# Preact convolution pair, one core: the work in front of the sampling loop in another order

## The chip, the core and the metric

The kernel runs on one core of a Trainium2 chip. Its time is the device time of one execution in microseconds (us), the median of several executions. The engines that matter are TensorE (PE), VectorE (DVE), ScalarE (ACT), GpSimd (POOL) and SyncE (SP, which here only issues DMAs). Each engine runs its own instructions strictly in the written order; they meet through semaphores.

## The reference

Two residual blocks on x of shape 4 x 128 x 32 x 32 (images, channels, rows, columns), in float32. Only the first concerns the change:

```python
def _gn(v, G=32, eps=1e-05):              # group norm without weights, 32 groups
    g = v.reshape(B_, G, C_ // G, H_, W_)
    m = jnp.mean(g, axis=(2, 3, 4), keepdims=True)
    s = jnp.var(g, axis=(2, 3, 4), keepdims=True)
    return ((g - m) / jnp.sqrt(s + eps)).reshape(v.shape)

x = x + _L0_conv_ref(_gn(x), ...)         # deformable 3x3 convolution, group norm of 16 groups
x = x + _L1_conv_ref(_gn(x), ...)         # two ternary 3x3 convolutions with batch norm

# inside _L0_conv_ref, x being the normalised input:
om = _conv2d(x, w_off, b_off, STRIDE, PAD)            # 27 channels: 9 taps x (y, x, mask)
off_y, off_x, m = jnp.split(om, 3, axis=1)
mask = jax.nn.sigmoid(m)
...                                                   # 4 bilinear corners, 9 taps, every pixel
out = jnp.einsum('bckhw,ock->bohw', sampled * mask[:, None], weight.reshape(Cout, Cin, KK))
```

## The kernel before

**Stages.** In front of the loop, up to about 41 us of the trace, the kernel loads x, normalises the four images, computes the offset convolution and writes the transposed images to DRAM (tensor xt), so that small patches of them can be fetched. Then a loop of 36 slots, 9 a image, samples and applies the deformable weights; then come the second block's convolutions. The change is in the first stage alone; nothing of the loop or of what follows it is written differently.

**Precision.** A float32 operand is split in a high part that TensorE takes as it is (xhi, wdhi, woffT part 0) and a low part, the rest (xlo, wdlo, woffT part 1); products of the pairs are added. So each image needs `heads` (ACT writes xhi from x, scale and shift), `whole` (the normalised image xb, on ACT for images 0 and 1; `whole_late`, on DVE, for 2 and 3), and the low part xlo = xb - xhi (`tails` on DVE, semaphore xlo_ok; for image 3 `low_parts(3)` on POOL, semaphore xlo_pool).

**Statistics.** For image b, DVE computes `image_stats` (two halves of 512 columns with BN_STATS, L1455, and one BN_AGGR, L1463). TensorE adds the channels of a group with a product by a constant matrix (`group_mean`, L693). DVE turns this into deviations (`deviation`, L1413 to L1408), TensorE adds again (`group_square`, L698), ACT takes the root (`root`, L1099), and DVE makes scale and shift (`scale_shift`, L1433 to L1448). Images 2 and 3 share one such round, named by 2. PE's products for the means stand between those of the offset convolution, at places that the table `SUMS` gives.

**Offset convolution.** `offset_part(b, h, part)`, for image b and its half h, is 6 products of 512 columns on xhi (part 0) or 3 on xlo (part 1), all L741. ACT adds the bias (`tail`, tile omc, L1127), PE turns the result so that pixels lie on partitions (`turn_offsets`, 24 small transposes, L767), DVE adds three rows of it (`offsets`, tile omr, L1833), ACT takes the sigmoid of the masks (`masks`, L1139), SP copies omr to the neighbouring partitions (`replicate`, semaphore rep_in), and POOL makes from it the distances (tile hat, L562 and L565), which ACT clips (`hats`, L1144 and L1146), and their outer product vt (`outer`, L575 and L581), one for each slot of the loop. The waits of an offset_part:

```python
if (b, h, part) == (0, 0, 0):
    pe.wait_ge(xhi_top, 1)
elif not part:
    pe.wait_ge(xhi_ok, b + 1)
elif b == 0:
    pe.wait_ge(xlo_first, 1)
elif b == 3:
    pe.wait_ge(xlo_pool, 1)
else:
    pe.wait_ge(xlo_ok, b)
```

**Images to DRAM.** `turn_image(b)` (PE, L718) transposes xb, `pixels_hi(b)` (ACT, L1134) and `pixels_lo(b)` (DVE, L1828) split it into xtv, SP stores it.

**Weights.** PE turns the 9 taps of the offset weights (L680) and of the deformable ones (`turn_deformable`, L688, wd_raw); ACT and DVE split these (`deformable_hi`, `deformable_lo`, tiles wdhi and wdlo, L1803).

**The first products.** As soon as POOL has written the identity matrix, PE runs `keep_going(6)`, six products of the identity with itself (L672), whose result nobody reads; one more stands behind each of the first two group sums.

**Who orders the work.** Everything is an order written by hand, engine by engine. PE's, from image 1 on: offset_part(1,0,0) with both sums of images 2 and 3 in it, turn_offsets(0), offset_part(1,0,1), turn_image(1), offset_conv(1,1), turn_image(2), offset_conv(2,0), turn_offsets(1), turn_image(3), offset_conv(2,1), offset_conv(3,0), and then the first outer products. The sums of all images share one PSUM bank with the output of offset_part(1,1,0), which therefore waits for the scale_shift of images 2 and 3 (gn_var).

Of the kernel before, what the change touches and what calls it, by code (L numbers as in the profile page):

```python
# [20 lines left out]
BIG = 512  # L21
# [36 lines left out]
def build(nc, x, w_off, b_off, wd, bias, gamma, beta, w1, g1, be1, w2, g2, be2, out):  # L58
# [8 lines left out]
    with ExitStack() as ctx:  # L67
# [432 lines left out]
        def _(pool):  # L500
# [47 lines left out]
            def low_parts(b):  # L548

                pool.wait_ge(xn_late, b - 1)  # L550
                pool.wait_ge(xhi_ok, b + 1)
                g.tensor_tensor(inner(xlo, b), square(plain(b)), inner(xhi, b), ALU.subtract).then_inc(xlo_pool, 1)
# [74 lines left out]
            for n in range(-5, CHUNKS):  # L627
                if 0 <= n + 3 < CHUNKS:
                    outer(n + 3)
                if n + 5 < CHUNKS:  # L630
                    distances(n + 5)
                if n == -4:
                    low_parts(3)
                for i, level in FOLDED.get(n, ()):
# [31 lines left out]
        def _(pe):  # L666
            t = nc.tensor

            def keep_going(n):

                for _ in range(n):
                    t.matmul(PS[:, 5, 0:P], ident[:, :], ident[:, :], start=True, stop=True)  # L672

            pe.wait_ge(consts, 1)
            keep_going(6)
            pe.wait_ge(consts, 3)
# [76 lines left out]
            def turn_offsets(b):  # L753
# [5 lines left out]
                for step in range(K):  # L759
# [12 lines left out]
            SUMS = {(0, 0, 0): ((group_mean, 1, (2, 0)),), (0, 1, 0): ((group_square, 1, (0, 0)),),  # L772
                    (1, 0, 0): ((group_mean, 2, (0, 0)), (group_square, 2, (2, 1)))}

# [11 lines left out]
            offset_part(1, 0, 0)  # L786
            turn_offsets(0)
            offset_part(1, 0, 1)
            turn_image(1)
            offset_conv(1, 1)  # L790
# [286 lines left out]
        def _(act):  # L1077
# [224 lines left out]
            heads(GN0, 1)  # L1302
            whole(GN0, 1)
            tail(0)
            tail(1)
            pixels_hi(0)
            root(GN0, 2)
# [79 lines left out]
        def _(dve):  # L1387
# [422 lines left out]
            dve.wait_ge(x_in[1], 16)  # L1810
            image_stats(GN0, 1)
            deviation(GN0, 1)
            dve.wait_ge(xhi_ok, 1)
            dve.wait_ge(xn_ok, 1)
            d.tensor_tensor(inner(xlo, 0), square(plain(0)), inner(xhi, 0), ALU.subtract).then_inc(xlo_first, 1)
            scale_shift(GN0, 1)
            dve.wait_ge(x_in[2], 16)
            image_stats(GN0, 2, last=False)
            deformable_lo(0)
            dve.wait_ge(x_in[3], 16)  # L1820
            image_stats(GN0, 3)
            deformable_lo(1)
            deviation(GN0, 2)
            tails(GN0, 1)
# [10 lines left out]

            dve.wait_ge(pads, 11)
            deformable_lo(2)
            pixels_lo(0)
            offsets(0)
            offsets(1)  # L1840
            scale_shift(GN0, 2)
            whole_late(2)
# [151 lines left out]
```

## Time and profile before

| | |
|---|---|
| median of 3 executions | 272.83 us (272.41 to 274.51) |
| the profiled execution | 272.33 us, its span 270.6 us |
| TensorE busy | 244.2 us, 90% of the span |
| VectorE busy | 213.6 us, 79% |
| ScalarE busy | 171.9 us, 64% |
| GpSimd busy | 166.3 us, 61% |
| mean granted TensorE clock | 0.978 |

The time of an execution lies 1.7 us above the span, which runs from the first to the last instruction. Matmuls are pipelined, so a long busy time of PE says only that something stood in it; where a chain of waits runs through an engine, that engine sets the time there. Times of the trace count from the start of the span.

### The profile page before, as it was taken

The page shows a single profiled execution, that of the slowest core. Times are in us where ns is not written, and L with a number is a line of the kernel's source. Part 1 is how long each engine was busy: PE and PEld are TensorE (multiplying, and loading weights), DVE is VectorE, ACT ScalarE, POOL GpSimd, SP SyncE. Part 2 cuts the span into 40 slices and gives each one's busy share as a digit, 9 for nine tenths or more (in the row PEclk, how much of TensorE's full clock was granted, in tenths as well). Part 3 has the DMA queues.
Part 4 walks back from the last instruction along what each step waited for, and adds up shares of the span by engine and source line. Part 5 has one row for each costly group of instructions (what it writes and reads, how often), then busy time and mean ns, then how long its engine had stood idle before and what let it go on. Part 6 is the DMA issues. An engine that isn't in the chain of part 4 may idle for free.

```text
span 270.6 us, 5607 instructions
## 1 busy us (share of the span) xinstructions
PE 244.2 (90%) x1960; PEld 210.8 (78%) x1960; DVE 213.6 (79%) x473; ACT 171.9 (64%) x364; POOL 166.3 (61%) x217
## 2 busy tenths in 40 slices
PE   6989998999999899998998999899999999999800
PEld 6867666899988799897998888899987776777600
DVE  5599556989888999559979789985588787699493
ACT  2488756989779978877799778757216406630140
POOL 8000899999668788777668987486900601936051
PEclk9999999999999999999999999999999999999965
DMA  7925686544444422333323334300000000000016
GB/s 216 378 69 186 208 263 239 164 146 135 133 140 135 127 95 75 110 114 108 111 79 105 96 131 132 103 30 2 0 0 0 2 1 0 0 0 2 5 54 261
DMA packets 25593, 28.13 MB, mean 104 GB/s; under 512 B 2509, under 2 KB 23613, under 8 KB 25560
## 3 DMA queue, kind: packets, MB, share of 16 engines
q1 hardware_dynamic: 24912, 25.95, 29.3%
q10 hardware_dynamic: 648, 1.76, 1.8%
q8 instruction: 18, 0.29, 0.5%
q14 instruction: 15, 0.12, 0.1%
HBM read 19.87 MB, written 6.78 MB: 99 GB/s over the span
## 4 chain that ended last, share of the span: by engine, by line
PE 64%; DVE 22%; ACT 8%; issue 2%; DMA 1%; DVEq 0%
PE PS L949 13%; PE PS L855 6%; PE PS L741 5%; PE PS L808 5%; PE PS L857 5%; PE PS L856 5%; PE PS L837 5%; DVE slo L1556 5%; PE PS L984 4%; PE PS L838 4%; PE PS L839 4%; DVE vlo L1567 3%; DVE st L1455 3%; ACT vhi L1165 3%; PE PS L767 2%
## 5 line engine op out<-in xcount | busy, mean ns | idle before, releaser
L581 POOL TENSOR_TENSOR vt<-rowm,hat 128x1026 f32<-128x1026 f32 x36 | 70.8, 1966 | 25.9 <-PE PS L817 24.1
L1567 DVE TENSOR_TENSOR vlo<-PS,vhi 128x576 fp32r<-128x576 f32 (+2 forms) x88 | 50.1, 590 | 17.5 <-ACT vhi L1165 17.2
L1165 ACT ACTIVATE vhi<-PS 128x576 fp32r<-128x576 f32 (+2 forms) x88 | 43.8, 523 | 19.1 <-PE PS L839 19.0
L1556 DVE TENSOR_TENSOR slo<-PS,shi 114x512 fp32r<-114x512 f32 (+1 forms) x68 | 43.2, 675 | 6.3 <-ACT shi L1153 6.0
L855 PE MATMUL PS<-vhi,wdhi 128*128 128x256 f32 x144 | 43.4, 301 | 0.8 <-ACT xb L1172 0.7
L837 PE MATMUL PS<-shi,patch 114*128 114x288 f32 (+1 forms) x136 | 42.0, 309 | 1.0 <-DVE vlo L1567 0.6
L857 PE MATMUL PS<-vhi,wdlo 128*128 128x256 f32 x144 | 40.5, 281 | 0.0
L856 PE MATMUL PS<-vlo,wdhi 128*128 128x256 f32 x144 | 40.4, 281 | 0.0
L838 PE MATMUL PS<-slo,patch 114*128 114x288 f32 (+1 forms) x136 | 40.2, 296 | 0.0
L839 PE MATMUL PS<-shi,patch 114*128 114x288 f32 (+1 forms) x136 | 40.0, 294 | 0.0
L1153 ACT ACTIVATE shi<-PS 114x512 fp32r<-114x512 f32 (+1 forms) x68 | 36.7, 592 | 4.9 <-PE PS L808 4.4
L855 PEld LDWEIGHTS PS<-vhi,wdhi 128*128 128x128 f32 x144 | 27.5, 191 | 2.3 <-issue 1.1
L837 PEld LDWEIGHTS PS<-shi,patch 114*128 114x128 f32 x136 | 25.8, 190 | 2.2 <-issue 1.9
L856 PEld LDWEIGHTS PS<-vlo,wdhi 128*128 128x128 f32 x144 | 27.2, 189 | 0.1
L857 PEld LDWEIGHTS PS<-vhi,wdlo 128*128 128x128 f32 x144 | 27.1, 188 | 0.0
L838 PEld LDWEIGHTS PS<-slo,patch 114*128 114x128 f32 x136 | 25.9, 190 | 0.1
L839 PEld LDWEIGHTS PS<-shi,patch 114*128 114x128 f32 x136 | 25.8, 190 | 0.0
L562 POOL TENSOR_TENSOR hat<-omr,rtab 128x54 f32<-128x54 f32 x36 | 12.8, 357 | 20.8 <-DMA omr<-omr 20.8
L808 PE MATMUL PS<-ident,vt 64*114 64x64 f32 x536 | 23.5, 223 | 0.4 <-POOL vt L581 0.3
L808 PEld LDWEIGHTS PS<-ident,vt 64*114 64x114 f32 x536 | 18.6, 132 | 4.9 <-issue 2.7
L949 PE MATMUL PS<-xhi,q 128*128 128x512 f32 (+1 forms) x72 | 18.5, 406 | 0.9 <-ACT xhi L1264 0.6
L949 PE MATMUL PS<-xlo,q 128*128 128x512 f32 (+1 forms) x72 | 18.6, 406 | 0.0
(217 smaller groups left out, 518.0 us busy)
## 6 DMA issues: line engine op xcount, KB each, us to landing
patch<-xt SPq DMA_DIRECT2D x136, 114.0 KB
xt<-xtv SPq DMA_DIRECT2D x4, 1024.0 KB, 6.2
xs<-in_x SPq DMA_DIRECT2D x3, 512.0 KB, 7.5
wraw<-in_L_conv_w SPq DMA_DIRECT2D x2, 576.0 KB, 9.5
out<-xb SPq DMA_DIRECT2D x4, 256.0 KB, 2.6
wd_raw<-in_L_conv_weight ACTq DMA_DIRECT2D x1, 576.0 KB, 6.9
xs<-in_x SPq DMA_DIRECT2D x2, 256.0 KB, 4.1
omr<-omr SPq DMA_DIRECT2D x8, 64.0 KB, 4.5
```

The lines of the kernel that those rows point to most:

```text
L581: g.tensor_tensor(vt[:, n % 2, :, :].rearrange("p t (r j) -> p t r j", r=WR), rowm[:, n % 2, :, :].unsqueeze(3).to_broadcast([P, TAPS, WR, ...
L808: ins = t.transpose(S_PAIR[u][:, tap, :], vt[at, n % 2, tap, :], ident[at, at])
L837: t.matmul(v, patch[:, n % PATCHES, m, 0, :], hi[at], start=True, stop=False)
L838: t.matmul(v, patch[:, n % PATCHES, m, 0, :], lo[at], start=False, stop=False)
L839: last = t.matmul(v, patch[:, n % PATCHES, m, 1, :], hi[at], start=False, stop=True)
L855: t.matmul(O_PS, wdhi[:, w, :], hi, start=(tap == TAPS - 1), stop=False)
L856: t.matmul(O_PS, wdhi[:, w, :], lo, start=False, stop=False)
L857: last = t.matmul(O_PS, wdlo[:, w, :], hi, start=False, stop=(tap == 0))
L949: last = t.matmul(tap_out(PS[:, bank, :], h, k), q[:, k, :], tap_in(src, b, h, k), start=(i == 0 and part == 0), stop=(i == TAPS - 1 and p ...
L1165: last = a.activation(places(vhi), src, ACT.Copy)
L1556: d.tensor_tensor(lo, src, hi, ALU.subtract).then_inc(slo_ok, 1 if pairs(n) == 2 else 3)
L1567: last = d.tensor_tensor(places(vlo), src, places(vhi), ALU.subtract)
```

## The change

Seven edits, all in front of the loop:

1. PE: instead of six identity products, nine products of 512 columns with the tile woffT, which is still all zero then; they wait for DVE's memsets (semaphore zeroed) and no longer for POOL's identity.
2. DVE: the statistics of the first half of image 2 stand in front of `deviation(GN0, 1)`; only the second half stays behind `scale_shift(GN0, 1)`.
3. PE: the sum for the means of images 2 and 3 stands behind the sixth product of offset_part(1,0,0), not behind its first; the sum for the squares stands behind turn_offsets(0).
4. PE: turn_image(1) stands in front of offset_part(1,0,1).
5. ACT: `whole(GN0, 1)` stands behind tail(0) and tail(1).
6. DVE: deformable_lo(2) stands in front of `deviation(GN0, 2)`, and `scale_shift(GN0, 2)` in front of pixels_lo(0) and the two offsets.
7. POOL: low_parts(3) stands behind the first outer product, not in front of it.

```diff
                 if 0 <= n + 3 < CHUNKS:
                     outer(n + 3)
+                    if n == -3:
+                        low_parts(3)
                 if n + 5 < CHUNKS:
                     distances(n + 5)
-                if n == -4:
-                    low_parts(3)
...
-            pe.wait_ge(consts, 1)
-            keep_going(6)
+            zeros = woffT[:, :, :, :].rearrange("p l x c -> p (l x c)")
+            pe.wait_ge(zeroed, 4)
+            for _ in range(9):
+                t.matmul(PS[0:STACK, 5, :], zeros[:, 0:STACK], zeros[:, 0:BIG], start=True, stop=True)
             pe.wait_ge(consts, 3)
             pe.wait_ge(woff_in, 16)
...
             SUMS = {(0, 0, 0): ((group_mean, 1, (2, 0)),), (0, 1, 0): ((group_square, 1, (0, 0)),),
-                    (1, 0, 0): ((group_mean, 2, (0, 0)), (group_square, 2, (2, 1)))}
+                    (1, 0, 0): ((group_mean, 2, (2, 1)),)}
...
             offset_part(1, 0, 0)
             turn_offsets(0)
-            offset_part(1, 0, 1)
+            group_square(GN0, 2)
             turn_image(1)
+            offset_part(1, 0, 1)
             offset_conv(1, 1)
...
             heads(GN0, 1)
-            whole(GN0, 1)
             tail(0)
             tail(1)
+            whole(GN0, 1)
             pixels_hi(0)
             root(GN0, 2)
...
             image_stats(GN0, 1)
+            dve.wait_ge(x_in[2], 16)
+            half_stats(GN0, 2, 0)
             deviation(GN0, 1)
...
             scale_shift(GN0, 1)
-            dve.wait_ge(x_in[2], 16)
-            image_stats(GN0, 2, last=False)
+            image_stats(GN0, 2, last=False, halves=(1,))
             deformable_lo(0)
             dve.wait_ge(x_in[3], 16)
             image_stats(GN0, 3)
             deformable_lo(1)
+            dve.wait_ge(pads, 11)
+            deformable_lo(2)
             deviation(GN0, 2)
             tails(GN0, 1)
...
-            dve.wait_ge(pads, 11)
-            deformable_lo(2)
+            scale_shift(GN0, 2)
             pixels_lo(0)
             offsets(0)
             offsets(1)
-            scale_shift(GN0, 2)
             whole_late(2)
```

PE at image 1's first half, before: the two sums (mv, then nsm) stand in the convolution's six products.

```order
L741 MATMUL PS<-xhi,woffT 96x512 [waits wd_ok,xhi_ok]
L693 MATMUL PS<-mv,g 128x2 [waits gn_in]
L741 MATMUL PS<-xhi,woffT 96x512 x5
L698 MATMUL PS<-nsm,g 128x2 [waits gn_dev]
L767 MATMUL PS<-ident,omc 128x32 [waits off_tail,pads]
```

The same place of the changed kernel, whose line numbers are other ones:

```order
L743 MATMUL PS<-xhi,woffT 96x512 [waits wd_ok,xhi_ok]
L743 MATMUL PS<-xhi,woffT 96x512 x5
L695 MATMUL PS<-mv,g 128x2 [waits gn_in]
L769 MATMUL PS<-ident,omc 128x32 [waits off_tail,pads]
L769 MATMUL PS<-ident,omc 128x32 x7
```

The first sum has moved behind all six products, the second behind the 24 transposes that begin in the last two rows.

DVE from the low part of image 1 on, before: the third of the deformable weights, pixels_lo(0), the offsets, and then the six small steps of scale_shift for images 2 and 3.

```order
L1475 TENSOR_TENSOR xlo<-xb,xhi 128x32x32 [waits xn_ok,xhi_ok]
L1803 TENSOR_TENSOR wdlo<-PS,wdhi 128x384 [waits wd_hi,pads]
L1828 TENSOR_TENSOR xtv<-PS,xtv 128x8x128 [waits xthi_ok]
L1833 TENSOR_REDUCE omr<-PS 128x4x27 [waits off_t] x2
L1433 TENSOR_SCALAR nsm<-PS 128x2 [waits gn_std]
L1434 RECIPROCAL nsm<-nsm 128x2
L1438 TENSOR_TENSOR nsm<-nsm 128x2 [waits dch]
L1439 TENSOR_TENSOR nsm<-nsm 128x2 [waits dch]
L1446 SCALAR_TENSOR_TENSOR nsm<-nsm 128x2 [waits dch]
L1448 TENSOR_TENSOR nsm<-nsm 128x2 [waits dch]
```

The changed kernel from the same step on:

```order
L1478 TENSOR_TENSOR xlo<-xb,xhi 128x32x32 [waits xn_ok,xhi_ok]
L1436 TENSOR_SCALAR nsm<-PS 128x2 [waits gn_std]
L1437 RECIPROCAL nsm<-nsm 128x2
L1441 TENSOR_TENSOR nsm<-nsm 128x2 [waits dch]
L1442 TENSOR_TENSOR nsm<-nsm 128x2 [waits dch]
L1449 SCALAR_TENSOR_TENSOR nsm<-nsm 128x2 [waits dch]
L1451 TENSOR_TENSOR nsm<-nsm 128x2 [waits dch]
L1834 TENSOR_TENSOR xtv<-PS,xtv 128x8x128 [waits xthi_ok]
L1839 TENSOR_REDUCE omr<-PS 128x4x27 [waits off_t] x2
```

The six small steps now stand in front of the pixels and the offsets, and the weights' third has gone ahead of this stretch.

POOL at the start of its work for the loop, before: the last of the distances of two slots, the low part of image 3 (xlo), and the first outer product (rowm and vt).

```order
L565 TENSOR_TENSOR hat<-omr,ctab 128x171
L552 TENSOR_TENSOR xlo<-xb,xhi 128x32x32 [waits xhi_ok,xn_late]
L575 TENSOR_TENSOR rowm<-hat,omr 128x54 [waits hat_ok,hat_d]
L581 TENSOR_TENSOR vt<-rowm,hat 128x1026 [waits rowm_ok]
L562 TENSOR_TENSOR hat<-omr,rtab 128x54
```

The same place of the changed kernel:

```order
L565 TENSOR_TENSOR hat<-omr,ctab 128x171
L575 TENSOR_TENSOR rowm<-hat,omr 128x54 [waits hat_ok,hat_d]
L581 TENSOR_TENSOR vt<-rowm,hat 128x1026 [waits rowm_ok]
L552 TENSOR_TENSOR xlo<-xb,xhi 128x32x32 [waits xhi_ok,xn_late]
L562 TENSOR_TENSOR hat<-omr,rtab 128x54
```

The low part has moved behind the outer product. SP's order is the same in both.

## Rows read from the trace of the kernel before

**Rows 1.** Chain that ended last, 1 to 36 us: start us, us, what

```profile
8.81 2.19 PE PS L688 x9
11.00 1.28 PE PS L741 x3
...
31.05 4.34 PE PS L741 x18
```

**Rows 2.** Timeline of PE, front of the kernel: start us, us, instruction, idle before

```profile
1.98 2.93 PE L672 MATMUL PS<-ident 128*128 128x128 f32 x12 [1.98 <-POOL ident L509]
4.84 1.22 PE L680 MATMUL PS<-ident,woff_raw 27*128 27x27 f32 x9
6.43 0.59 PE L693 MATMUL PS<-mv,g 128*128 128x1 f32 x2 [0.37 <-DVE mv L1463]
...
18.36 0.38 PE L693 MATMUL PS<-mv,g 128*128 128x2 f32 x2 [0.69 <-DVE mv L1463]
...
20.10 1.48 PE L767 MATMUL PS<-ident,omc 32*128 32x32 f32 x24
...
22.31 1.04 PE L718 MATMUL PS<-ident,xb 128*128 128x128 f32 x8
...
26.19 1.70 PE L741 MATMUL PS<-xhi,woffT 128*96 128x512 f32 x6
...
34.51 0.88 PE L741 MATMUL PS<-xlo,woffT 128*96 128x512 f32 x3
```

**Rows 3.** Two stretches: us, busy of five engines, granted clock, DMA share, GB/s

```profile
41.00:50.00 9.00, 7.27 (x86) 5.70 (x86) 6.74 (x18) 6.40 (x19) 8.69 (x14) 1.00 0.62 214
...
259.00:262.00 3.00, 0.00 (x0) 0.00 (x0) 3.00 (x4) 2.16 (x4) 1.82 (x2) 0.50 0.00 0
```

**Rows 4.** The page, part 6: DMA issues, KB each, median us to landing

```profile
xs<-in_x SPq DMA_DIRECT2D x3, 512.0 KB, 7.5
```

**Rows 5.** Timeline of DVE

```profile
12.53 0.16 DVE L1413 TENSOR_SCALAR nsm<-PS 128x1 f32<-128x1 f32 x1 [1.40 <-PE PS L693]
...
14.93 1.28 DVE L1455 BATCH_NORM_STATS2 st<-xs 128x6 f32<-128x512 f32 x2
...
18.79 0.16 DVE L1413 TENSOR_SCALAR nsm<-PS 128x2 f32<-128x2 f32 x1
...
20.46 0.55 DVE L1803 TENSOR_TENSOR wdlo<-PS,wdhi 128x384 fp32r<-128x384 f32 x1
20.93 1.22 DVE L1828 TENSOR_TENSOR xtv<-PS,xtv 128x1024 fp32r<-128x1024 f32 x1
22.06 0.89 DVE L1833 TENSOR_REDUCE omr<-PS 128x108 f32<-128x324 f32 x2
22.86 0.15 DVE L1433 TENSOR_SCALAR nsm<-PS 128x2 f32<-128x2 f32 x1
...
23.90 0.81 DVE L1808 TENSOR_SCALAR xb<-xs,nsm 128x1024 f32<-128x1024 f32 x1
```

**Rows 6.** Timeline of ACT

```profile
9.41 1.53 ACT L1108 ACTIVATE xhi<-xs,nsm 128x544 fp32r<-128x544 f32 x2 [0.94 <-DVE nsm L1448]
...
22.98 0.27 ACT L1139 ACTIVATE omr<-omr 128x72 f32<-128x72 f32 x1 [1.00 <-DVE omr L1833]
...
24.63 1.24 ACT L1108 ACTIVATE xhi<-xs,nsm 128x1024 fp32r<-128x1024 f32 x1
...
29.40 0.39 ACT L1146 ACTIVATE hat<-hat 128x225 f32<-128x225 f32 x1
```

**Rows 7.** Timeline of POOL: its first work for the loop

```profile
28.22 0.28 POOL L562 TENSOR_TENSOR hat<-omr,rtab 128x54 f32<-128x54 f32 x1 [20.84 <-DMA omr<-omr]
...
29.58 2.21 POOL L552 TENSOR_TENSOR xlo<-xb,xhi 128x1024 fp32r<-128x1024 f32 x1
31.75 0.28 POOL L575 TENSOR_TENSOR rowm<-hat,omr 128x54 f32<-128x54 f32 x1
32.10 1.96 POOL L581 TENSOR_TENSOR vt<-rowm,hat 128x1026 f32<-128x1026 f32 x1
```

More of the change, by code:

```diff
@@ L787, in _ @@
             turn_offsets(0)
+            group_square(GN0, 2)
+            turn_image(1)
             offset_part(1, 0, 1)
-            turn_image(1)
             offset_conv(1, 1)
```

## Prediction

> **What bounds the kernel now.** I read the chain of waits first, since it says which engine's work the end hangs on in the stretch that the change touches. Up to 18.4 us it goes back and forth between DVE and PE; from there to 41 us it is PE alone, product behind product [rows 1]. So two things are worth time: whatever brings forward the moment at which PE's unbroken stretch begins, and whatever another engine could push into that stretch as a new wait. Next, PE's timeline: PE does no waiting worth naming but 0.69 us for the statistics of images 2 and 3 at 18.36 [rows 2]. The third thing to see is pace. Three products of 512 columns at 11.00 take 1.28 us, 0.427 each, which is 1.2 GHz; eighteen at 31.05 take 4.34, 0.241 each, which is near the 2.4 GHz level [rows 1]. So PE runs at the lower level until about 12.5 us and at the upper one from there. The view of stretches gives the granted clock as 1.00 from the start, as it has no record before the rise; the pace decides. Last, the queue of steps from DVE's offsets to the loop: masks on ACT, copies by SP, distances, hats, the low part of image 3 and the first outer product [rows 5 to 7].
>
> **The zero products (edit 1).** DVE's memsets end at about 1.6 us, some 0.4 before the identity. Nine products at 0.427 take 3.84 and end at 5.5, where the identity products ended at 4.91 [rows 1, 2]. The nine transposes behind them (1.22 us at the low level) then end by 6.7, or by about 6.3 if the clock has risen, against 6.06; the first group sum wants to start at 6.43 [rows 2], so the cost is 0 to 0.3. What they buy is the clock. Nothing in this trace shows how long zero products at full width need to raise it. What it shows: 2.9 us of identity products on 128 columns did not, and the unbroken stretch from 8.81 on did, before 13 us. The zero products are, like that stretch, wide products without a gap between them, so I take it that they raise the clock before the first group sum; the other outcome is the first rival. Then the sum at 6.43 and the one for the squares shrink from 0.59 to 0.38 each [rows 2], and the heads of image 0 start at 9.0, not 9.41 [rows 6]; the deformable weights' nine transposes, taken to start at 8.81 as before, need 1.1, not 2.19, and the offset convolution starts at 9.9, not 11.00 [rows 1].
>
> The Trainium skill, "TensorE: Matmul & The Clock Gate", Part 1, says that a throttled clock is the default, that activity releases it, and that the moment shifts from run to run; the trace agrees as far as it has a late rise, and by that rule a single run may fall on either side of my sum.
>
> **Half of image 2's statistics, early (edit 2).** DVE has finished image 1's statistics at 11.13 and waits 1.40 for PE's sum [rows 5]. In the changed kernel these end at 10.7 (the 0.4 from above), PE has its three products done by 10.6 and the sum by 11.1; DVE does the half (0.64, half of 1.28 [rows 5]) in that wait and starts image 1's deviation at 11.3, not 12.53: 1.2 earlier. It needs image 2's x, the second of three loads with 7.5 to landing [rows 4]; SP issues it near 2.2, so it is there at about 9.7, a microsecond of cover; were it gone, every microsecond would come on top. Behind it, DVE's work up to the statistics of image 3 is shorter by that 0.64: they are ready at 16.5, not 18.3.
>
> **Means later (edit 3).** PE's own stream is 1.5 earlier by then (the sum 1.3, and two products that ran before the rise). The first product of image 1 ended at 17.67 [18.36 less the wait of 0.69, rows 2]; now it ends at 16.1, the sixth at 17.3, the sum at 17.5. So PE no longer waits for the statistics; DVE waits for PE, and spends the wait on two thirds of the deformable weights (edit 6, 0.42 each, free). Its deviation starts at 17.55, not 18.79 [rows 5]: 1.24 earlier, and the low part of image 1 with it.
>
> **Scale and shift in front of the pixels (edit 6).** This one costs. In PE's order the square sum now stands behind the 24 transposes: 17.4 plus 1.4 plus 0.25 [rows 2] is 19.05, ACT's root ends at 19.35. DVE is free at 20.46 - 1.24 = 19.2, waits 0.15, takes 1.04 for the six steps (22.86 to 23.90), and starts the pixels at 20.45; before it did the last third of the weights there (0.47) and started them at 20.93 [rows 5]. The offsets end at 22.45 and not at 22.95: of 1.24 there is 0.5 left. What waits behind the six steps is what leads out of the first stage: masks, SP's copies (SP's order is unchanged, but they are its first long wait), and POOL.
>
> **ACT's tails before whole(1), turn_image(1) before the low products (edits 4, 5).** The tails are ready to read at 15.2 and 15.9, whole(1) ends at 17.8, and DVE wants it at 18.1: free, and if that 0.3 of cover went, DVE would be late by what is missing. PE's swap fills the time until the low part of image 1 is there (19.3) with 1.04 of transposes [rows 2]: free.
>
> **POOL (edit 7).** Masks 0.5 earlier, so distances at 27.7 and hats at 29.3 (28.22 and 29.79 [rows 6, 7]). Before, the low part of image 3 lay in the wait for the hats and was done at 31.79, when PE wanted it only at 34.51 [rows 2, 7]. Now the outer product goes first: 29.35 plus 0.35 plus 1.93 is 31.6, plus 2.21 is 33.8 [rows 7]. PE itself gets there at 33.7: image 2's heads end 0.5 earlier, at 25.4, and PE, which took up image 2 at 26.19, runs the same 8.32 us from there to the low products of image 3 [rows 2, 6]. So PE waits 0.15 for POOL and goes on at 33.85 instead of 34.51.
>
> **Sum.** 34.51 - 33.85 = 0.65 us less. Of the larger gains upstream (1.24 at DVE's deviation) the rest is given back to the six small steps and to POOL's new order. Beyond, the first outer product is ready (31.6, wanted at 34.7), and what follows hangs on PE, so I let it shift as a whole. Bounds: 0.4 if POOL's spans, which are rough, are 0.25 longer; 0.8 if POOL does not hold PE and image 2's heads alone do (26.19 - 25.4). The profiled execution took 272.33, so 271.7; it lay 0.5 under the median of the runs, from which it would be 272.2. I give 271.8.
>
> **Rivals.** *The zeros raise nothing (slower).* The clock rises where it did. Then the zero products' 0.6 delays the first sum by 0.3, and all up to DVE's first deviation; the early half still wins 0.64, but PE, at its old pace, reaches the means only at 19.4; DVE's deviation is 0.6 late, the square sum ends at 20.9, the root at 21.2, the pixels start at 22.3 instead of 20.93. Offsets end 1.35 later, and POOL's low part at 29.79 + 1.35 + 0.04 + 2.28 + 2.21 = 35.7: PE goes on 1.15 later, 273.5. It decides at the offsets: the low part ends 11.4 after them, so past 23.1 us the new order loses. For it: identity products did not help either. Against: the clock's rise at full load.
>
> On the same page, under "Seeing it yourself", the Trainium skill says of another throttle, the limiter of peak current, that operands of all zeros do not trip it. No run here shows whether the gate of the clock looks at data; if it did, this rival would hold, 273.5.
>
> *The clock rises late, or falls again.* From 5.5 to 8.8 PE has little to do. At the kernel's end the clock is down to 0.50 when PE has nothing left, while from 41 to 50, where PE waits here and there (7.27 of 9 us busy), it held [rows 3]; which of the two this stretch resembles I cannot read from the rows. If it rises only near 9.3, or falls there and comes back as before, DVE's first deviation is 0.6 to 0.8 later than in my sum and all behind it too: 0 to 0.35 slower than before, 272.3 to 272.7.
>
> *The early part counts in full.* PE is through with image 1's transposes and low products at 20.7, where both were done at 23.35 [rows 2]: 2.6 us. If neither image 2's heads nor the low part held it, 269.7. Against it are the two waits above, both behind the same offsets.
>
> **How the numbers follow.** Chances: the sum 0.55, late or lost clock 0.22, zeros without effect 0.15, the full gain (or most of it) 0.05, else 0.03. The range from 270.9 to 273.3 holds the first two with the 0.5 between profile and median on both sides, and leaves out the last three for the most part. One per cent, 2.7 us, is about what a measurement of this kernel can tell from no change: faster by more needs the full gain, 0.05; slower by more needs more than twice the slow rival, 0.03; within it 0.92.
>
> **What would show it.** Right: products of 512 columns at 0.24 from the first one on, near 9.9; DVE's idle of 1.40 gone; the six small steps at 19.4 and the offsets done by 22.5; a short wait of PE on POOL's xlo at 33.8. Wrong: a first product at 11 or later, 0.43 each; offsets done after 23.1; a wait of PE on ACT's heads or on POOL of more than a microsecond; or a PE that is over 1.5 us ahead at the first outer product.

## The result, and the profile after

The changed kernel takes 274.12 us in the median (20 executions, 273.02 to 275.32), beside 272.95 for the kernel before (20 executions on the same chip, 272.10 to 274.62). The ratio is 1.0039, its 95% interval 1.0020 to 1.0057. So the change cost about 1.1 us; the forecast was 271.8, and 274.12 lies above its range as well. The profiled execution took 273.77, which is 1.44 more than the one of before (272.33); its span is 271.9.

The chain that ended last, changed kernel (start us, us, what), answers to [rows 1]:

```profile
9.19 2.19 PE PS L690 x9
11.38 1.06 PE PS L743 x3
...
20.70 0.27 ACT nsm L1102
20.97 0.02 issue
20.99 0.16 DVE nsm L1436
...
33.20 2.23 POOL xlo L552
35.43 0.04 issue
35.48 0.96 PE PS L743 x3
```

Before, it was PE alone from 18.4 us to 41. Now it leaves PE at 20.7, goes over ACT's root and DVE's six small steps to the offsets, on to POOL's low part of image 3, and comes back to PE at 35.48. That is the path the forecast had drawn, only 1.6 us later than drawn.

PE's timeline, changed kernel, answers to [rows 2]:

```profile
3.48 2.10 PE L677 MATMUL PS<-woffT 128*96 128x512 f32 x5
5.50 1.21 PE L682 MATMUL PS<-ident,woff_raw 27*128 27x27 f32 x9
6.64 0.38 PE L695 MATMUL PS<-mv,g 128*128 128x1 f32 x2
...
9.19 2.19 PE L690 MATMUL PS<-ident,wd_raw 128*128 128x128 f32 x9 [0.89 <-DMA wd_raw<-in_L_conv_weight]
11.03 1.40 PE L743 MATMUL PS<-xhi,woffT 128*96 128x512 f32 x3
...
18.65 0.28 PE L695 MATMUL PS<-mv,g 128*128 128x2 f32 x2
...
26.91 1.72 PE L743 MATMUL PS<-xhi,woffT 128*96 128x512 f32 x6 [1.10 <-ACT xhi L1111]
```

The first group sum takes 0.38, as forecast for the upper clock; the nine transposes of the deformable weights take 2.19, the lower one's duration, and the convolution starts at 11.03 and not at 9.9. So the clock was up at 6.64 and down again at 9.19. The view of stretches says the same (us, busy of five engines, granted clock, DMA share, GB/s):

```profile
5.20:8.50 3.30, 2.87 (x19) 2.15 (x17) 1.54 (x7) 0.64 (x2) 2.19 (x9) 1.00 0.99 399
8.60:11.90 3.30, 2.71 (x11) 2.54 (x12) 2.79 (x8) 2.66 (x3) 0.00 (x0) 0.50 1.03 424
...
46.20:49.50 3.30, 3.27 (x14) 2.82 (x13) 2.25 (x6) 2.75 (x7) 3.14 (x5) 0.50 0.56 193
```

The trace's clock records put a rise at 5.17 us, a fall at 8.58, a rise at 11.99, and a second dip inside the loop, from 46.1 to 49.5. The kernel before has one rise, at 12.7, and holds it until 258.45, past the end of its last product (256.01).

DVE's timeline, changed kernel, answers to [rows 5]:

```profile
10.85 0.64 DVE L1458 BATCH_NORM_STATS2 st<-xs 128x6 f32<-128x512 f32 x1
12.59 0.16 DVE L1416 TENSOR_SCALAR nsm<-PS 128x1 f32<-128x1 f32 x1 [1.10 <-PE PS L695]
...
18.97 0.16 DVE L1416 TENSOR_SCALAR nsm<-PS 128x2 f32<-128x2 f32 x1 [0.40 <-PE PS L695]
...
20.99 0.16 DVE L1436 TENSOR_SCALAR nsm<-PS 128x2 f32<-128x2 f32 x1 [0.26 <-ACT nsm L1102]
...
21.92 1.22 DVE L1834 TENSOR_TENSOR xtv<-PS,xtv 128x1024 fp32r<-128x1024 f32 x1
23.06 0.89 DVE L1839 TENSOR_REDUCE omr<-PS 128x108 f32<-128x324 f32 x2
```

The early half of the statistics did go into DVE's wait (10.85), and yet DVE still waits 1.10 behind it: PE's sum is not there. The deviation of image 1 is at 12.59 (12.53 before), that of images 2 and 3 at 18.97 (18.79 before), and then the offsets are done at 23.95 where before they were done at 22.95.

**Where the 1.44 us went.** Deviation of images 2 and 3: 0.18 late. From there to the end of the offsets: 4.98 where before it was 4.16, so 0.82 more; 1.00 late in all. PE's low products of image 3 at 35.48 against 34.51: 0.97 late. Up to the first deformable products of the loop (53.55 against 52.17) another 0.41, in the second dip of the clock. The last product of PE (its end 257.45 against 256.01): 1.44 late.

### The profile page after: what moved, and what is told of

The parts are those of the page before. It is cut to its first block, busy times and chain, and to the rows that moved or that the text cites. A ratio compares the mean times of both kernels' runs of the same rounds, so it can differ in the third digit from the quotient of the medians.

```text
span 271.9 us, 5601 instructions
## 1 busy us (share of the span) xinstructions
PE 245.2 (90%) x1957; PEld 210.3 (77%) x1957; DVE 213.6 (79%) x473; ACT 172.3 (63%) x364; POOL 166.5 (61%) x217
## 4 chain that ended last, share of the span: by engine, by line
PE 60%; DVE 19%; ACT 9%; DMA 3%; issue 3%; POOL 1%; SPq 1%; ACTq 0%; POOLq 0%; DVEq 0%
PE PS L952 13%; PE PS L858 6%; PE PS L811 5%; PE PS L860 5%; PE PS L859 5%; PE PS L840 4%; PE PS L987 4%; PE PS L841 4%; PE PS L842 4%; DVE slo L1559 4%; PE PS L743 3%; ACT vhi L1168 3%; DMA wd_raw<-in_L_conv_weight 3%; DVE vlo L1570 3%; ACT shi L1156 2%
## 5 line engine op out<-in xcount | busy, mean ns | idle before, releaser
L840 PE MATMUL PS<-shi,patch 114*128 114x288 f32 (+1 forms) x136 | 42.6, 313 | 0.5 <-DVE omr L1839 0.3
L841 PE MATMUL PS<-slo,patch 114*128 114x288 f32 (+1 forms) x136 | 40.8, 300 | 0.0
L842 PE MATMUL PS<-shi,patch 114*128 114x288 f32 (+1 forms) x136 | 40.5, 298 | 0.0
L840 PEld LDWEIGHTS PS<-shi,patch 114*128 114x128 f32 x136 | 26.2, 193 | 1.8 <-issue 1.6
L842 PEld LDWEIGHTS PS<-shi,patch 114*128 114x128 f32 x136 | 26.4, 194 | 0.0
L952 PE MATMUL PS<-xhi,q 128*128 128x512 f32 (+1 forms) x72 | 18.4, 406 | 0.9 <-ACT xhi L1267 0.6
```

The source lines that it names most:

```text
L840: t.matmul(v, patch[:, n % PATCHES, m, 0, :], hi[at], start=True, stop=False)
L841: t.matmul(v, patch[:, n % PATCHES, m, 0, :], lo[at], start=False, stop=False)
L842: last = t.matmul(v, patch[:, n % PATCHES, m, 1, :], hi[at], start=False, stop=True)
L952: last = t.matmul(tap_out(PS[:, bank, :], h, k), q[:, k, :], tap_in(src, b, h, k), start=(i == 0 and part == 0), stop=(i == TAPS - 1 and p ...
```

## The experiments

Two theories were open. *The clock:* the zero products raise it too soon, it falls over the small work that follows, and so the forecast's early gain never comes; what is left is the cost of the edits that give time back. *The new order:* scale_shift in front of the offsets, and POOL's low part behind the outer product, cost more than they bring, whatever the clock. All kernels are edits of the changed kernel, except one of the kernel before; where a text says that edit 6 is undone, its six steps go back behind the offsets, and the weights' third stays where the change put it. Each was timed in 12 executions; the kernel before that shares their runs had 272.66 to 273.18 in the median. The times at the events below are those of each one's profiled execution.

**1. scale_shift(GN0, 2) behind the offsets again.**

```diff
-            scale_shift(GN0, 2)
             pixels_lo(0)
             offsets(0)
             offsets(1)
+            scale_shift(GN0, 2)
```

> Changed kernel, but the six steps of scale_shift for images 2 and 3 stand behind pixels_lo(0) and the two offsets again. Theory A (order: those steps, 1.0 us, sit in front of the offsets and everything that leads out of the first stage hangs on the offsets): offsets end at 23.0 instead of 23.95, the heads of image 2 at 25.9, PE reaches the low products of image 3 at 34.5 instead of 35.5; time 1.0 us under the changed kernel, a ratio to the kernel before of 1.000. Theory B (a later fall of the clock, at 46 us in the changed kernel's profile, makes the difference, the order none): ratio stays at 1.004. Theory C (POOL's new order is what costs): the ratio stays above 1.003.

Measured: 272.94 us, ratio to the kernel before 0.9995 (0.9959 to 1.0031); PE's low products of image 3 at 34.23. DVE's timeline of this kernel:

```profile
18.96 0.16 DVE L1416 TENSOR_SCALAR nsm<-PS 128x2 f32<-128x2 f32 x1 [0.39 <-PE PS L695]
...
20.64 1.22 DVE L1834 TENSOR_TENSOR xtv<-PS,xtv 128x1024 fp32r<-128x1024 f32 x1
21.77 0.89 DVE L1839 TENSOR_REDUCE omr<-PS 128x108 f32<-128x324 f32 x2
```

The deviation stands where it stood in the changed kernel (18.96 and 18.97), and the offsets end at 22.66 and not at 23.95. With the clock doing the same thing in both (5.3 up, 8.8 down, 12.2 up here), the place of the six steps alone is worth 1.28 us between deviation and offsets (3.70 against 4.98), where the theory had 1.0. Of this the steps themselves are 0.93 (20.99 to 21.92 in the changed kernel); the rest is DVE's wait for ACT's root, which hangs on the sum that edit 3 put behind the 24 transposes. The ratio shows no loss any more, though its interval still overlaps that of the changed kernel.

**2. The same edit alone, in the kernel before:** scale_shift(GN0, 2) in front of pixels_lo(0) and the offsets, nothing else.

> Kernel before, with one edit of the change alone: scale_shift for images 2 and 3 in front of pixels_lo(0) and the offsets. Theory A (those six steps in front of the offsets are the cost): offsets end at 24.0 instead of 22.95, image 2's heads at 26.9, PE takes up image 2 at 26.95 instead of 26.19, and from there everything is 0.75 us later; POOL's low part, still in the wait for the hats, holds nobody. Time +0.75 us, ratio 1.0025 to 1.003. Rival (the cost is in the other moves or in the clock): ratio 1.000.

Measured: 273.26 us, ratio 1.0017 (0.9997 to 1.0038), profiled 274.01. The interval holds the ratios of both expectations, so the trace has to decide. From deviation (19.84) to the end of the offsets (24.92) it is 5.08, where before it was 4.16: 0.92 more, which is the six steps without a wait for the root. The deviation itself is 1.05 late, which the edit has no part in: 0.43 of it was there at image 1's deviation already (12.96 against 12.53; PE had waited 0.65 for the weights' DMA and began their transposes at 9.24, not 8.81), and the rest came while the clock was still down, since it rose only at 14.6 in this execution. The 1.7 between the two profiled times is therefore not the edit's alone. That is the first sign that two profiled executions can't be set side by side to a microsecond here.

**3. POOL's low part in front of the first outer product again** (edit 7 undone).

> Changed kernel, but POOL's low part of image 3 in front of its first outer product again. Theory C (POOL's order is what costs): PE's low products of image 3 at 34.5, time 1.0 us under the changed kernel, ratio 1.000. Theory A (the offsets are late, and PE has waited 1.1 us for the heads of image 2 before it comes to POOL's part): PE comes to these products at 35.3 by itself, so only 0.2 us is won, ratio 1.003 to 1.004; the first outer product is done at 35.1, just in time.

Measured: 273.73 us, ratio 1.0027 (1.0000 to 1.0055). POOL's timeline of this kernel:

```profile
30.59 2.22 POOL L552 TENSOR_TENSOR xlo<-xb,xhi 128x1024 fp32r<-128x1024 f32 x1
```

and PE's:

```profile
26.95 1.71 PE L743 MATMUL PS<-xhi,woffT 128*96 128x512 f32 x6 [1.10 <-ACT xhi L1111]
...
35.28 0.89 PE L743 MATMUL PS<-xlo,woffT 128*96 128x512 f32 x3
```

POOL is done at 32.81, 2.6 us earlier than in the changed kernel, and PE begins at 35.28 and not at 35.48. It had taken up image 2 at 26.95, after 1.10 of waiting for its heads, and ran its own 8.33 from there. Edit 7 costs 0.2 us in these traces, since two paths from the same offsets arrive almost together.

**4. Edits 6 and 7 both undone,** the reordered front alone.

> The changed kernel with edits 6 and 7 both undone (scale and shift behind the offsets, POOL's low part before the first outer product), the reordered front left. Theory (6 costs about 1.0 us at the offsets, 7 costs 0 to 0.3): offsets end near 22.7, PE goes on with image 3's low part near 34.0, time 272.5 to 272.9, 0 to 0.4 below the kernel in which edit 6 alone is undone. Rival (the two edits are worth their cost, the reordered front costs): 273.5 or more.

Measured: 273.53 us, ratio 1.0002 (0.9970 to 1.0035); offsets end at 22.60, PE's low products of image 3 at 34.20. Against the first experiment (22.66, 34.23) edit 7 is worth nothing that shows. The events are those of the theory (22.7, 34.0); the median is the rival's 273.5, but the kernel before stood at 273.18 in the same runs, and the ratio decides for neither. The reordered front is shown to be neither faster nor slower than the kernel before.

**5. Six identity products in place of the nine zero products** (edit 1 undone).

```diff
-            zeros = woffT[:, :, :, :].rearrange("p l x c -> p (l x c)")
-            pe.wait_ge(zeroed, 4)
-            for _ in range(9):
-                t.matmul(PS[0:STACK, 5, :], zeros[:, 0:STACK], zeros[:, 0:BIG], start=True, stop=True)
+            pe.wait_ge(consts, 1)
+            keep_going(6)
```

> Changed kernel, but with the six identity products of before in place of the nine zero products. Theory A (the clock that the zeros raise at 5.2 is lost again at 8.6, before the work that needed it): the clock rises once, after 11 us; the first sum starts at 6.4 but is slow; offsets end at 23.9 to 24.2 and the ratio is 1.003 to 1.005, that is, the zeros bring or cost at most 0.2 us. Theory D (the zeros themselves cost, by delaying the first sum or by an earlier fall of the clock later): ratio 1.000 to 1.002.

Measured: 274.24 us, ratio 1.0039 (1.0011 to 1.0066), the same ratio as with the zeros. And in this profiled execution the identity products raised the clock, at 5.0, and it fell at 8.4 and came back at 11.8, where the theory had one rise after 11; the offsets end at 23.52. So zeros are not needed to raise it: either kind can, and whether the clock then holds is another matter.

**6. Neither:** no products at all ahead of the offset weights' transposes.

> Changed kernel without the nine zero products and without the identity products that stood there before: PE does nothing until the offset weights are in. Theory A (whatever raises the clock at 5 us, it is lost before the stretch that needs it): the clock rises once, between 11 and 14 us, offsets end at 23.8 to 24.4, ratio 1.003 to 1.006, as for the changed kernel. Rival (the early clock is worth the 0.4 us and more of the prediction): ratio 1.006 or more, offsets after 24.5.

Measured: 274.29 us, ratio 1.0076 (1.0036 to 1.0117); the clock rises at 13.3, offsets end at 24.31, profiled 273.63. This comes close to the first rival's case (24.30 and 273.5). The ratio is the one that its rival expected (1.006 or more), the offsets are the theory's (23.8 to 24.4). The interval overlaps that of the changed kernel, so what the zeros bring beside nothing is not settled by the times.

**7. A filler for the gaps:** wide zero products in place of the two short identity products, two behind the first group sum and five behind the second.

```diff
...
             group_mean(GN0, 0)
-            keep_going(1)
+            keep_wide(2)
             group_square(GN0, 0)
-            keep_going(1)
+            keep_wide(5)
...
```

> Changed kernel, with two wide zero products behind the first mean and five behind the first square sum in place of one identity product each, on a tile of its own that is zeroed first; nothing else. It tests the sum of the prediction: the clock is to be held from 5 us on. Prediction's theory: the offset convolution's products run at 0.24 us from the first on, near 10; the means of image 1 at 11.2 to 11.5; offsets end at 22.5 to 22.8; PE reaches the low products of image 3 at 33.9 to 34.2; time 1.3 to 1.6 us under the changed kernel, ratio 0.998. Rival (the order costs whatever the clock): offsets still end after 23.5, ratio over 1.002.

Measured: 273.81 us (272.04 to 275.44), ratio 1.0018 (0.9985 to 1.0051). In the profiled execution the clock did not rise before 11.2, though the nine zero products ran as before; the filler then ran at the lower clock, and the weights' transposes began at 10.8. The theory could not be tested in this one: there was no raised clock to hold.

**8. Means earlier still:** edits 3, 5, 6 and 7 undone; PE's sum of image 1's means in front of the convolution, that of its squares behind the third product.

```diff
-            SUMS = {(0, 0, 0): ((group_mean, 1, (2, 0)),), (0, 1, 0): ((group_square, 1, (0, 0)),),
-                    (1, 0, 0): ((group_mean, 2, (2, 1)),)}
+            SUMS = {(0, 0, 0): ((group_square, 1, (2, 0)),),
+                    (1, 0, 0): ((group_mean, 2, (0, 0)), (group_square, 2, (2, 1)))}
...
             pe.wait_ge(pads, 6)
+            group_mean(GN0, 1)
...
```

> Changed kernel with the steps undone that cost (scale and shift behind the offsets, POOL's low part in front of the outer product, whole(1) in front of the tails) and PE's sums put where DVE has just made them: the mean of image 1 in front of the offset convolution, its square behind the third product, the means of 2 and 3 behind the first product of image 1 and their square behind the sixth. Theory A, second half (DVE's row of steps up to the offsets sets the pace, and it waits 1.1 us for PE's mean of image 1 and 0.4 for that of 2 and 3): image 1's deviation at 11.5 instead of 12.6, the deviation of 2 and 3 at 17.8 instead of 19.0, offsets end at 21.3 to 21.8, PE takes up image 2 at 24.9 to 25.3, goes on with image 3's low products at 33.3 to 33.8; time 0.7 to 1.1 us under the kernel before, ratio 0.996 to 0.9975. Rival (the clock sets the pace): ratio 1.000, as for e1_ss_back.

Measured: 273.19 us, ratio 0.9999 (0.9975 to 1.0023). The clock rose only at 17.3 in the profiled execution and x came late (first group sum at 7.25), so its events (offsets 24.42) say nothing of the order. The ratio is the one that the rival expected (1.000).

**9. The same with a filler** of one and three wide products.

> e8_means_early with one wide zero product behind the first mean and three behind the first square sum in place of one identity product each. If the clock is up by 6 us and is held until 12, the offset convolution's first products run at 0.24 and PE is done with image 1 some 0.5 us earlier; since the sums no longer stand behind these products, offsets end at most 0.3 us earlier than in e8_means_early; time 0 to 0.4 us under it, ratio 0.995 to 0.997. If the clock is not held in the profiled execution, as e8_means_early.

Measured: 272.96 us (270.81 to 274.39), ratio 0.9981 (0.9952 to 1.0010). The clock rose at 6.0, fell at 9.4 and rose at 12.8. The early means worked: image 1's deviation at 11.91, offsets end at 22.00, PE's low products of image 3 at 33.96, 0.55 ahead of before. And the profiled execution took 274.39, since PE's first deformable products came at 54.27, 2.10 behind before. Its view of stretches shows why:

```profile
43.60:53.70 10.10, 9.66 (x53) 8.50 (x54) 7.33 (x17) 6.48 (x16) 9.43 (x15) 0.50 0.57 185
53.90:60.00 6.10, 6.10 (x71) 5.80 (x65) 4.29 (x8) 4.82 (x11) 5.91 (x8) 1.00 0.50 152
```

The clock was down for ten microseconds in the loop: from PE's low products of image 3 to the first deformable ones it is 20.31 us, beside 17.66 before. That took 2.65 us, almost five times what the front had won.

**10. The changed kernel with a denser filler,** three and six wide products.

> The changed kernel with nine wide zero products as filler in place of two short identity products: three behind the first group sum of image 0, six behind the second, so that PE has columns to stream up to the weights' transposes at 9.2 us. Theory (the term of edit 1 failed because the clock fell at 8.6 us; held up, the prediction's terms come back): an execution that rises by about 6 us and stays up has the deviation of image 1 near 11.3 us, offsets end at 22.3 to 22.6, and a time of 271.6 to 272.3; an execution in which it rises late has PE behind the filler by about 2 us, offsets end near 24.5 and 273.8 to 275. The median lies between, wherever the two mix, so the lowest times and the profile count. Rival (edit 6 costs its 1.0 us whatever the clock): no execution below 273.0, offsets end not before 23.3 even where the clock stays up.

Measured: 274.17 us (272.35 to 276.05), ratio 1.0020 (0.9982 to 1.0058). PE's timeline of this kernel:

```profile
9.00 2.85 PE L708 MATMUL PS<-q 128*96 128x512 f32 x6
11.65 2.12 PE L690 MATMUL PS<-ident,wd_raw 128*128 128x128 f32 x9
```

and its view of stretches up to the rise, in which 1.00 stands as long as there is no record:

```profile
4.00:13.50 9.50, 9.50 (x37) 7.10 (x35) 5.09 (x16) 3.29 (x5) 3.40 (x13) 1.00 1.00 375
```

The clock rose at 13.7 only, though PE was shown busy without a gap, and the filler, 0.47 each, put everything back by 2.5 us (offsets end at 26.04, profiled 275.93; the theory had 24.5 and at most 275 for a late rise). Four of the twelve executions lie below 273.0 (272.35 to 272.90), which the rival ruled out. A filler is a bet on the early rise.

**11. The same filler, and scale_shift behind the offsets again.**

> The same filler, and scale and shift of image 2 and 3 behind the offsets again. Theory: with the clock held the offsets end at 21.3 to 21.8 us, 1.0 earlier than in the kernel with the filler alone, and the time is 271.2 to 272.0; with a late rise about 23.4 and 273 to 274. Rival (an early end of the offsets is not worth its length, since the clock falls again later in the kernel): offsets end at 21.5 but the time stays at 272.5 to 273.5, with a second fall between 40 and 55 us.

Measured: 273.19 us (271.10 to 275.51), ratio 0.9980 (0.9948 to 1.0013). In this profiled execution, 271.10, the clock rose at 4.7 and held to 257.3. The view of stretches:

```profile
4.70:8.50 3.80, 3.71 (x22) 2.68 (x21) 1.82 (x9) 0.64 (x2) 2.69 (x9) 1.00 0.97 382
8.60:11.90 3.30, 3.30 (x21) 2.52 (x20) 3.08 (x11) 2.65 (x3) 0.00 (x0) 1.00 1.03 422
```

PE's timeline:

```profile
1.66 3.70 PE L677 MATMUL PS<-woffT 128*96 128x512 f32 x9 [1.66 <-DVE eps L1410]
...
9.21 1.24 PE L690 MATMUL PS<-ident,wd_raw 128*128 128x128 f32 x9
10.21 0.97 PE L751 MATMUL PS<-xhi,woffT 128*96 128x512 f32 x3
...
21.63 1.68 PE L751 MATMUL PS<-xhi,woffT 128*96 128x512 f32 x6 [0.57 <-DVE nsm L1445]
```

and DVE's:

```profile
11.34 0.16 DVE L1425 TENSOR_SCALAR nsm<-PS 128x1 f32<-128x1 f32 x1
...
17.72 0.16 DVE L1425 TENSOR_SCALAR nsm<-PS 128x2 f32<-128x2 f32 x1 [0.22 <-PE PS L695]
...
19.40 1.22 DVE L1843 TENSOR_TENSOR xtv<-PS,xtv 128x1024 fp32r<-128x1024 f32 x1
```

The forecast had 1.1 for the transposes (1.24 here), 11.3 for image 1's deviation (11.34), and 17.55 for that of images 2 and 3 (17.72): held up, the clock brings the early terms. The offsets end at 21.42, 1.53 ahead of before, and the time is 1.23 below before's profiled one. The wait of 0.57 at 21.63 is what edit 6 takes away in PE, and it costs less than edit 6 does. The median, 273.19, is still that of the kernel before in the same runs (273.18); whether its longer executions are those with a late rise, as in the tenth experiment, their times alone can't show.

**12. The changed kernel with all its edits, the filler of three and six, and eleven zero products instead of nine.**

> The changed kernel with the filler of three and six wide products and eleven zero products at its start in place of nine, all seven edits in place. Two products more cost 0.5 us where the clock is already up and 0.9 where it is not. Theory (with the clock held from 5 to 12 us the terms of the prediction hold; edit 6 then costs 1.0 and leaves the rest): an execution in which it rises by 6 and stays up has the deviation of image 1 at 11.3 to 11.6 us, offsets end at 22.4 to 22.7, PE at the low part of image 3 at 33.9 to 34.2, and 271.7 to 272.2. An execution with a late rise: 274 to 276. Rival (the changed order costs whatever the clock): offsets end at 23.3 or later even with the clock up, and 273 or more.

Measured: 273.18 us (272.55 to 274.21), ratio 1.0016 (0.9993 to 1.0038), profiled 272.55. Here the clock rose at 4.9 and held to 260.9, with edit 6 in place. The view of stretches:

```profile
5.00:8.40 3.40, 3.40 (x21) 2.52 (x20) 1.38 (x6) 0.43 (x2) 2.41 (x9) 1.00 0.97 391
8.60:11.90 3.30, 3.30 (x22) 2.55 (x21) 3.12 (x12) 2.36 (x4) 0.00 (x0) 1.00 1.03 422
...
46.20:49.50 3.30, 2.45 (x27) 1.73 (x26) 3.09 (x8) 3.18 (x9) 3.14 (x6) 1.00 0.41 144
```

DVE's timeline:

```profile
11.75 0.16 DVE L1425 TENSOR_SCALAR nsm<-PS 128x1 f32<-128x1 f32 x1
...
18.13 0.16 DVE L1425 TENSOR_SCALAR nsm<-PS 128x2 f32<-128x2 f32 x1 [0.21 <-PE PS L695]
...
20.14 0.16 DVE L1445 TENSOR_SCALAR nsm<-PS 128x2 f32<-128x2 f32 x1 [0.26 <-ACT nsm L1110]
...
22.21 0.89 DVE L1848 TENSOR_REDUCE omr<-PS 128x108 f32<-128x324 f32 x2
```

and PE's:

```profile
1.66 4.24 PE L677 MATMUL PS<-woffT 128*96 128x512 f32 x11 [1.66 <-DVE eps L1410]
...
26.07 1.72 PE L751 MATMUL PS<-xhi,woffT 128*96 128x512 f32 x6 [1.10 <-ACT xhi L1119]
...
34.63 0.96 PE L751 MATMUL PS<-xlo,woffT 128*96 128x512 f32 x3
```

Beside the eleventh experiment everything up to the deviations is 0.41 later, the two zero products more. From there to the end of the offsets (18.13 to 23.10) it is 4.97, beside 3.70: 1.27 for the place of the six steps, the same as at the lower clock. The offsets end at 23.10, the break-even point that the forecast's rival had named (23.1), and PE's low products of image 3 begin at 34.63, 0.12 behind before; the time is 0.22 behind before's profiled one. The numbers fall between the two expectations: 0.40 above the theory's 22.7 for the offsets, which left no room for the 0.41 of the two products, and 0.20 below the rival's 23.3. Each is right in one half: with the clock up the early terms came, and edit 6 took its 1.27 out of them all the same.

## Why the prediction was wrong, by its own steps

| | forecast | changed kernel | clock held (12th; in brackets 11th) |
|---|---|---|---|
| weights' transposes, nine | 1.1 | 2.19 | 1.19 (1.24) |
| first offset convolution | 9.9 | 11.03 | 10.58 (10.21) |
| deviation of image 1 | 11.3 | 12.59 | 11.75 (11.34) |
| deviation of images 2 and 3 | 17.55 | 18.97 | 18.13 (17.72) |
| from there to the end of the offsets | 4.90 | 4.98 | 4.97 (3.70, edit 6 undone) |
| from there to PE's low products of image 3 | 11.4 | 11.53 | 11.53 (11.59) |
| these begin | 33.85 | 35.48 | 34.63 (33.01) |

- **The step that failed is "The zero products (edit 1)"**, in its second half. That they raise the clock before the first group sum came true in this execution (5.17; the sum took 0.38), with some luck: in three of the nine profiled executions with these nine products it rose only at 11.2 to 17.3. That it would still be up for the weights' transposes and the convolution was taken for granted there, and it was down from 8.58 to 11.99. Beside the eleventh experiment, in which the transposes began at the same moment (9.21, here 9.19), the first product of the convolution is 0.82 late and both deviations 1.25: this is what the fall cost. (The step had also taken the transposes to start at 8.81 as before. They hang on the weights' DMA, and where PE waited for it they started anywhere from 8.66 to 9.36; in the eleventh experiment, at 9.21, the deviation of image 1 came at the forecast's time all the same.) Between the nine wide products and the transposes stands PE's smallest work: nine transposes of 27 columns, four sums of one column, four short products, and a wait of 0.89 for the weights' DMA. The forecast had named this gap ("from 5.5 to 8.8 PE has little to do"), in a rival with a chance of 0.22.
- **That rival had the mechanism and not its price.** It gave 0 to 0.35 us; its event came to 1.0 at the offsets. It took DVE's first deviation to be 0.6 to 0.8 late against the sum. It was 1.3 late (12.59 against 11.3), and nothing behind it caught up: the deviation of images 2 and 3 was 1.42 late. On top of that came the cost of edit 6, which the sum had counted. The 273.77 of the profiled execution lies 2.1 above the sum's 271.7: 1.63 of it is there at PE's low products of image 3 (35.48 against 33.85), 0.41 came in the second dip, which no step of the prediction had.
- **"Half of image 2's statistics" and "Means later"** stood on the clock. With it they came within 0.2 us (11.34, 17.72). Without it the early half only shortened a wait that still ended with PE's sum, and "Means later" became a loss: PE, at 18.65, was behind the 18.36 of [rows 2].
- **"Scale and shift in front of the pixels"** was sized right: 4.90 forecast, 4.98 measured. The judgement was off: it was the only term that surely cost, at either clock, and it was paid from gains that hung on the clock. Undone, no loss shows in the ratio (0.9995).
- **"POOL (edit 7)"** was right: outer product first, PE goes on 11.5 after the offsets, and POOL holds PE by 0.2.
- **The first rival** (the clock rises where it did, 273.5) is nearly met by the sixth experiment, which has no zeros at all: offsets 24.31, 273.63. The changed kernel had its result by another way. The Trainium skill, "TensorE: Matmul & The Clock Gate", "Seeing it yourself", says of the limiter of peak current that zero operands don't trip it; that the gate of the clock takes zeros for no work, as that rival would have it, is refuted here, since in the twelfth experiment PE ran nothing but zero products from 1.66 until the rise at 4.9.

With the clock held and nine zeros, the change would have its offsets at 22.69, 0.26 ahead of before, and PE's low products of image 3 at 34.22, 0.29 ahead: an estimate from the twelfth experiment less the 0.41 of its two products. So even then the sum (0.5 ahead at the offsets, 0.65 at PE) was too good by 0.24 and 0.37: 0.17 lay ahead of the deviation of images 2 and 3, 0.08 between it and the offsets, and 0.13 between these and PE.

The mean granted clock of each execution says something of those without a profile. It counts the time before the first rise as full (in the kernel before, the fall at 258.45 alone makes its 0.978), and the profiled executions sort by it: 0.978 to 0.983 in the seven whose clock did not fall between its first rise and PE's last product, 0.971 to 0.976 in the five with one such fall, 0.955 and 0.968 in the two with two. Of the changed kernel's 20 executions 18 show 0.976 or less, so by this estimate they had at least one fall, as the profiled one had; of the kernel before, 17 of the 35 timed beside the first experiment. Of the twelfth experiment it is none of 12 (0.977 to 0.982), but of the tenth and the eleventh, with the same filler and nine zero products, 6 and 8 of 12. Whether such a fall lay in the front or in the loop, and when the clock first rose, the mean doesn't tell.

What stays open: why a second dip comes inside the loop in some executions, and, as far as the means can't say it, which clock each unprofiled execution had. That the filler is what held the clock, and not the earlier moment of the rise, rests on two profiled executions; their rises (4.7 and 4.9) were the earliest of all, though the one at 5.0, in the fifth experiment, was followed by a fall. No kernel tried is shown to beat the one before: 0.9980 (0.9948 to 1.0013) and 0.9981 (0.9952 to 1.0010) are the lowest ratios, and both intervals reach above 1.

## What to carry to other kernels

Work that is to warm a clock is worth something only if the work behind it keeps the clock up: look at what stands between the filler and the first stretch that is to be fast, and count a gain that hangs on it as one draw, not as a term. Keep apart the terms that hold at either clock (here 1.28 us for six small steps, and the wait in front of them, ahead of a long chain) from those that don't, and don't pay for the second kind with the first. Where a clock's moment wanders by microseconds, compare intervals inside one trace (deviation to offsets, offsets to PE's low products), which repeated to 0.01 to 0.1 us in kernels of the same order here, and not two total times.

## What the runs showed of the hardware

- The moment of the first rise wandered over the profiled executions from 4.7 to 17.3 us; with the same nine zero products at the start it was 4.7 to 6.0 in six, 11.2, 13.7 and 17.3 in three; with the six identity products 5.0, 12.7 and 14.6. In the tenth experiment PE was shown busy for all of the 9.50 us from 4.0 on, ahead of the rise at 13.7. The Trainium skill, "TensorE: Matmul & The Clock Gate", Part 1, gives half a microsecond to either side for it; the runs differ.
- The clock fell at 8.58 after a stretch in which PE was busy 2.87 of 3.30 us, in which the longest idle time that an instruction ended was 0.24; the wait for the weights had lasted 0.27 when it fell. The Trainium skill, on the same page under "HAM oscillation", lays a fall to the gaps in which PE waits for transfers; this one came over many small instructions. Of the eight executions with a rise by 6.0 us, six fell so. In the other two, those of the eleventh and the twelfth experiment, nine wide products stood in the same places (PE busy 3.71 of 3.80 and 3.40 of 3.40 us); with four of them, in the ninth, it fell.
- Inside the loop it fell in three of the profiled executions (46.1 to 49.5, 47.9 to 51.3, 43.5 to 53.8), where the kernel before and the twelfth experiment kept it from 46.2 to 49.5 with PE idle for a quarter of that stretch or more (busy 2.33 and 2.45 of 3.30). From PE's low products of image 3 to the first deformable ones it was 18.07, 18.20 and 20.31 us in these three, beside 17.66 in the kernel before: a dip cost from 0.4 to 2.65 us.
